# The gate/up loop of the last feed-forward: Silu and the up product one group apart, the up scale folded into the row maximum

## The reference, cut to what matters

```python
def _act_quant(x):
    scale = 127.0 / jnp.clip(jnp.max(jnp.abs(x), axis=-1, keepdims=True), 1e-05)
    xq = jnp.clip(jnp.round(x * scale), -128.0, 127.0) / scale
    return xq
...
gate = jax.nn.silu(_bitlinear(x, w_gate))     # x: 2048 x 1024, w: 4096 x 1024
up = _bitlinear(x, w_up)
g = _silu(_bitlinear(gate * up, w_down))      # w_down: 1024 x 4096
x = x + s * g
```

## Time and profile before

| | us |
|---|---|
| median of two runs | 6970.99 |
| the two runs | 6939.39, 7002.58 |
| profiled execution | 6944.18 |
| its span on the slowest core (core 0) | 6942.6 |
| spans of the eight cores | 6880.7 to 6942.6 |
| stage P9 in it, from 4256 to the end | 2687 |

### The profile page before, as it was taken

The page is one execution under the profiler, slowest core; times in us unless marked ns, Lnnn a source line. Parts: engine busy times, 40 slices in busy tenths (PEclk is TensorE's granted clock), DMA queues, the critical chain, the costliest instruction groups (busy, mean ns, idle before and its releaser), DMA issues.

```text
span 6942.6 us, 51492 instructions; the slowest of 8 cores (6880.7 to 6942.6 us)
## 1 busy us (share of the span) xinstructions
PE 2878.7 (41%) x14444; PEld 1414.7 (20%) x14539; DVE 3893.9 (56%) x5192; ACT 944.2 (14%) x1715; POOL 101.6 (1%) x140
## 2 busy tenths in 40 slices
PE   1455553777710000566666765150505050413221
PEld 0122221333300000132111113140404040313121
DVE  5444435111146567125766664867685959585866
ACT  0000000111101110005555550000000000000000
POOL 0000000000000000000000000000000000000000
PEclk6777766888855555787777778685857585857665
DMA  3200001876667651110000004231313140504131
GB/s 97 43 7 7 13 6 26 124 117 120 125 185 233 210 181 49 27 22 5 19 7 19 19 7 125 70 110 51 116 45 120 41 136 25 161 20 141 49 100 40
DMA packets 360992, 523.49 MB, mean 75 GB/s; under 512 B 21744, under 2 KB 257296, under 8 KB 352528
## 3 DMA queue, kind: packets, MB, share of 16 engines
q1 hardware_dynamic: 268496, 417.43, 19.0%
q0 software_dynamic: 92224, 102.77, 9.6%
HBM read 566.26 MB, written 50.33 MB: 89 GB/s over the span
## 4 chain that ended last, share of the span: by engine, by line
DVE 44%; PE 28%; DMA 16%; issue 6%; ACT 3%; DVEq 1%; SPq 1%; POOL 0%; ACTq 0%; POOLq 0%
DVE sb_BF L1797 7%; DVE sb_BF L1802 7%; PE ps L1392 5%; PE ps L1590 3%; DVE sb_STAT L1433 3%; DMA sb_BF<-s_sp 3%; PE ps L1407 2%; PE ps L1237 2%; DMA sb_BF<-wu0T 2%; PE ps L548 2%; PE ps L1438 2%; DMA sb_FW<-wd1T 2%; PE ps L924 2%; PE ps L916 2%; DMA sb_FW<-wg1T 2%
## 5 line engine op out<-in xcount | busy, mean ns | idle before, releaser
L1684 PE MATMUL ps<-sb_BF 128*128 128x256 bf16 x2048 | 500.1, 287 | 1639.1 <-DVE sb_SCR L1709 1267.5
L1684 PEld LDWEIGHTS ps<-sb_BF 128*128 128x128 bf16 x2048 | 210.1, 103 | 1722.7 <-issue 1689.6
L1419 ACT ACTIVATE sb_BF<-ps 128x512 bf16<-128x512 f32 x1024 | 525.7, 596 | 249.6 <-PE ps L1407 249.3
L1797 DVE SCALAR_TENSOR_TENSOR sb_BF<-sb_BF,sb_FW 128x2048 bf16<-128x2048 bf16 x224 | 513.4, 2292 | 23.6 <-DVE sb_BF L1802 0.5
L1802 DVE SCALAR_TENSOR_TENSOR sb_BF<-sb_BF 128x2048 bf16<-128x2048 bf16 x224 | 513.4, 2292 | 23.3
L1692 PE MATMUL ps<-sb_BF 128*128 128x256 bf16 x2048 | 499.2, 287 | 0.0
L1392 PE MATMUL ps<-sb_BF 128*65 128x512 bf16 x1024 | 411.5, 433 | 22.5 <-ACT sb_BF L1419 13.9
L1706 ACT ACTIVATE sb_SCR<-sb_SCR 128x256 f32<-128x256 f32 x256 | 106.6, 416 | 1957.5 <-DVE sb_SCR L1701 1957.5
L548 PE MATMUL ps<-sb_BF 128*128 128x512 bf16 x1002 | 242.5, 394 | 313.7 <-DMA sb_BF<-wkT 118.8
L916 PE MATMUL ps<-sb_BF 128*128 128x512 bf16 x736 | 298.3, 405 | 146.1 <-DMA sb_BF<-wu0T 54.3
L1590 PE MATMUL ps<-sb_BF 128*128 128x256 bf16 x2048 | 232.5, 275 | 209.3 <-DVE sb_BF L1806 207.2
(11 more groups left out here) (172 smaller groups left out, 4420.3 us busy)
## 6 DMA issues: line engine op xcount, KB each, us to landing
sb_BF<-wgq_sc SPq DMA_DIRECT2D x64, 1024.0 KB, 5.8
sb_BF<-wuq_sc SPq DMA_DIRECT2D x64, 1024.0 KB, 8.7
sb_BF<-wdq_sc SPq DMA_DIRECT2D x32, 2048.0 KB, 14.2
sb_FW<-wg1T SPq DMA_DIRECT2D x32, 1024.0 KB, 6.4
sb_FW<-wu1T SPq DMA_DIRECT2D x32, 1024.0 KB, 6.6
sb_FW<-wd1T SPq DMA_DIRECT2D x64, 512.0 KB, 3.7
sb_FW<-x SPq DMA_DIRECT2D x96, 256.0 KB, 6.1
sb_BF<-wg0T POOLq DMA_DIRECT2D x24, 1024.0 KB, 10.6
```

The source lines that it names most:

```text
L1419: e.activation(ring[rsl], self.bank(bsl, TT), AF.Exp, scale=0.125),
L1684: par=par, c0=c0, last=last: e.matmul(self.bank(bg, TQ), g_s[par][:, k * 512 + mh * 128: k * 512 + (mh + 1) * 128], xq[k][:, c0:c0 + TQ], ...
L1797: e.scalar_tensor_tensor(gbuf, rbuf, sbit, u, ALU.add, ALU.is_le),
```

## The change

Four things change in the loop and its tail.

- Silu of a group and the rest of its VectorE work are one group apart. After the matmuls of group `hh`, VectorE scales its gate half (now line 1729), ScalarE starts Silu, and VectorE turns to group `hh - 1`: it multiplies the up half straight from PSUM by the Silu result (L1676), takes the absolute value (L1682) and folds it into the maximum (L1686). `flush_h` holds these three. Scratch tiles are doubled, in free columns of `MU`.
- The up scale `cu` is no longer multiplied in per group. It is the same for all hidden features of a token, so it is applied once to the row of maxima (L1776), and to the reciprocal (L1785). Only one partition of it is computed.
- The reciprocal is taken on one partition of 256 columns (L1782) in place of 128, and is broadcast together with the maxima by a matmul of 512 columns (L1790). `rec_h` becomes a copy (L1800).
- The weight loads wait for TensorE's last matmul on the buffer, no longer for VectorE's maximum.

```diff
+        self._p9_vp = [0, 0]
...
+            pend = {}
+
+            def flush_h(hh):
+                bu, s_tt = pend.pop(hh)
+                self.drain("vector")
+                self.wait("vector", "se", s_tt)
+                vp = self.emit("vector", lambda e, hh=hh, bu=bu:
+                               e.tensor_tensor(
+                                   hpt[hh], self.bank(bu, TQ),
+                                   sl_s[hh % 2], ALU.mult), inc="ve")
+                self.release_bank(bu, "ve", vp)
+                self._p9_vp[hh % 2] = vp
+                self.drain("vector")
+                self.emit("vector", lambda e, hh=hh: e.scalar_tensor_tensor(
+                    vab, hpt[hh], -1.0, hpt[hh], ALU.mult, ALU.max),
+                    inc="ve")
+                self.drain("vector")
+                self.emit("vector", lambda e: e.tensor_tensor(
+                    mxh, mxh, vab, ALU.max), inc="ve")
+                self.drain("vector")
...
-                    self.wait("sync", "ve", g_cons[par])
+                    self.wait("sync", "te", g_cons[par])
...
-                    self.emit("vector", lambda e, bg=bg: e.tensor_tensor(
-                        scrq, self.bank(bg, TQ), cg, ALU.mult), inc="ve")
-                    v_t = self.milestone("vector", "ve")
-                    self.release_bank(bg, "ve", v_t)
-                    self.wait("scalar", "ve", v_t)
-                    s_tt = self.emit("scalar", lambda e: e.activation(
-                        scr2, scrq, AF.Silu), inc="se")
-                    self.wait("vector", "se", s_tt)
-                    self.emit("vector", lambda e, bu=bu: e.tensor_tensor(
-                        scrq, self.bank(bu, TQ), cu, ALU.mult), inc="ve")
-                    v_t = self.milestone("vector", "ve")
-                    self.release_bank(bu, "ve", v_t)
...
+                    vg = self.emit("vector", lambda e, bg=bg, hh=hh:
+                                   e.tensor_tensor(
+                                       sl_g[hh % 2], self.bank(bg, TQ),
+                                       cg, ALU.mult), inc="ve")
+                    self.release_bank(bg, "ve", vg)
+                    self.wait("scalar", "ve", vg)
+                    if self._p9_vp[hh % 2] > 0:
+                        self.wait("scalar", "ve", self._p9_vp[hh % 2])
+                    s_tt = self.emit("scalar", lambda e, hh=hh: e.activation(
+                        sl_s[hh % 2], sl_g[hh % 2], AF.Silu), inc="se")
+                    pend[hh] = (bu, s_tt)
+                    if (hh - 1) in pend:
+                        flush_h(hh - 1)
+                g_cons[par] = self.cnt["te"]
                 if tq > 0 and hs % 2 == 1:
                     emit_down_strip(tq - 1, hs // 2)
+            for hh in sorted(pend):
+                flush_h(hh)
...
+            self.emit("vector", lambda e: e.tensor_tensor(
+                mrow2, mrow, cu0, ALU.mult), inc="ve")
+            self.drain("vector")
             self.emit("vector", lambda e: e.tensor_single_scalar(
-                mrow, mrow, 1e-5, ALU.max), inc="ve")
+                mrow2, mrow2, 1e-5, ALU.max), inc="ve")
+            self.drain("vector")
+            self.emit("vector", lambda e: e.reciprocal(rfrow, mrow2),
+                      inc="ve")
+            self.drain("vector")
+            self.emit("vector", lambda e: e.tensor_tensor(
+                rfrow, rfrow, cu0, ALU.mult), inc="ve")
...
-                self.bank(0, TQ), self.ONEC[0:1, :], mrow,
+                self.bank(0, 2 * TQ), self.ONEC[0:1, :],
+                self.MU[0:1, 1024:1024 + 2 * TQ],
...
-            v_t = self.emit("vector", lambda e: e.reciprocal(
-                rec_h, self.bank(0, TQ)), inc="ve")
+            v_t = self.emit("vector", lambda e: e.tensor_copy(
+                rec_h, self.bank(0, TQ, off=TQ)), inc="ve")
```

More of the change, by code:

```diff
@@ L191, in build @@
         self.FW = sb("FW", [P, 8192], F32)
-        self.MU = sb("MU", [P, T], F32)
+        self.MU = sb("MU", [P, max(T, 1792)], F32)
         self.RS = sb("RS", [P, T], F32)
@@ L1554, in P9_l1_ffn @@
         mrow = self.MU[0:1, 0:TQ]
+        mrow2 = self.MU[0:1, 1024:1024 + TQ]
+        rfrow = self.MU[0:1, 1280:1280 + TQ]
         scrq = self.SCR[:, 0:TQ]
         scr2 = self.SCR[:, 256:512]
+        sl_g = [self.SCR[:, 0:TQ], self.MU[:, 512:768]]
+        sl_s = [self.SCR[:, 256:512], self.MU[:, 768:1024]]
+        vab = self.MU[:, 1536:1536 + TQ]
+        cu0 = self.STAT[0:1, 256:256 + TQ]
         NS = L1_HID // 512
@@ L1656, in P9_l1_ffn @@
             self.emit("vector", lambda e, c0=c0: e.tensor_scalar(
-                cu, self.SXR[:, c0:c0 + TQ], self.mclip[:, 1:2], 1.0 / 127.0,
-                ALU.mult, ALU.mult), inc="ve")
+                cu0, self.SXR[0:1, c0:c0 + TQ], self.mclip[0:1, 1:2],
+                1.0 / 127.0, ALU.mult, ALU.mult), inc="ve")
             self.drain("vector")
```

## The result

| | before | changed |
|---|---|---|
| median, us | 6944.55 (10 runs) | 7026.14 (11 runs) |
| lowest to highest, us | 6935.67 to 7021.08 | 7014.96 to 7046.57 |
| profiled execution, us | 6944.18 | 7018.84 |

The ratio is 1.0104, with a 95% interval of 1.0077 to 1.013: slower by 1%, within the 2% that count as no change. The forecast was 7020 us, a ratio of 1.011 on the profiled base. Some executions of a kernel take longer, with a lower granted clock on the four cores of one die; where that made over 1% (one execution each of experiments 1, 2 and 4), the execution is left out of the medians.

What follows compares the result with a forecast made beforehand. It took VectorE's chain to set the last stage's loop step, with TensorE having slack. Loop 69, first block -3, weights -6 and tail 16 sum to +76 us on 6944: 7020 us, 8 in 10 within 6960 to 7100.

Steps and rivals of the forecast that it cites:

- (a): Loop, VectorE: one multiplication less and Silu hidden; if VectorE set the step, it would fall from 3.23 to 2.26 us.
- (b): Loop, bank release: the late product stops TensorE from running ahead, so the step is 3.18 us against 3.23.
- overlap rival: Loop: TensorE still overlaps because the bank release is not where it was read; about 6720 us, chance 0.06.
- (c): Loop, down strips of 64 matmuls: no longer hidden by TensorE's lead, a step across one takes 8.73 us against 5.91.
- (d): Block start, clock: groups 2 and 3 run slow at 3.6 and 2.8 us, giving steps of 4.89 and 4.08.
- (e): Block loop in total: 9.8 us longer with strips, 69 us in seven blocks; the first block 3 us shorter.
- signs named for being right: Trace signs expected if the forecast held; the one judged is loop windows of about 123 us with strips.
- (f): Loop, weight loads: issued earlier against their use, giving back 6 us (0 to 8).
- (g): Tail once per block: new reciprocal, multiplications and wider broadcast add 2.0 us, eight times 16 us.
- clock rival: Loop: TensorE, waiting between groups, falls to 1.2 GHz, 3.6 us a group instead of 1.90; about 7130 us, chance 0.11.
- no-change rival: Loop: strips stay as hidden as before, with steps of 3.18 and 5.9 us; 6962 us, chance 0.08.

Runs made afterwards that it cites:

- experiment 1: Changed kernel with each group's product right behind its own gate scaling, ahead of VectorE's next wait for TensorE; 6830.8 us, 0.982 of the kernel before.
- experiment 2: Changed kernel with a group's gate and up halves sharing one bank, so four groups are in flight instead of two; 6765.7 us, 0.974 of the kernel before.
- experiment 4: Changed kernel with eight of a down strip's 64 matmuls behind each group, not all in one piece; 6905.1 us, 0.994 of the kernel before.
- experiment 6: Changed kernel with the weight loads waiting for VectorE's maximum again; 7037.9 us, 1.011 of the kernel before.
- experiment 8: Changed kernel with four groups in flight and the down strips spread over the groups; 6785.2 us, 0.975 of the kernel before.
- third experiment: Changed kernel without the one-group lag, each group finished before the next and Silu in the open; 6909.8 us, 0.992 of the kernel before.

## Why the prediction was right

- *(a), (b), the step.* Forecast 3.18, measured 3.18 to 3.19 in nearly every step. Each link is there: 0.60 from gate scaling to product, 0.42 for the product, 1.90 for the group, and 0.26 for the two handovers. Experiments 1 and 2 take away the late release, or what it costs, in two ways and give back 195 and 260 us on the medians. The overlap rival is refuted in the changed kernel and is what the experiments build; with the changed kernel's two buffers it comes to 6831 us (experiment 1) and not to its 6720, since the strip step stays 8.73.
- *(c), the strips.* Forecast 8.73, measured 8.73 in all 21 such steps; experiment 4 confirms it by removing them.
- *(d), the start of a block.* Partly wrong. Group 2 took 3.4 to 3.6 us, as forecast, but group 3 ran at full clock in six of seven blocks, though I had taken 2.8. The first step was 0.34, not 0.60: between two gate scalings stands only a wait for TensorE, already met.
- *(e), the loop.* From a block's first gate scaling to group 31's first matmul: 112.1 to 112.7 us in six blocks and 114.3 in one (group 3 slow), mean 112.6, against 104.1 before. Times seven, 60 us; the forecast had 69 - 6 = 63. One of the signs named for being right does not fit: from first gate scaling to last maximum a loop takes 118.6 us in the mean against 112.0, and not about 123. The 9.8 us counted to group 31's first matmul, and VectorE follows that by 2.0 us now and by 4.9 before.
- *(f), the loads.* Close in its sum. The loop before does have late weights, in one block above all (the fourth): TensorE idles 3.84 us ahead of group 12 and 4.47 ahead of group 20, and both groups then take 3.6 us.

```profile
5265.90 0.37 PE L1684 MATMUL ps<-sb_BF 128*128 128x256 bf16 x1 [3.84 <-DVE sb_SCR L1701]
```

The view names VectorE, but the banks had been free since 5263.24 (the end of group 10's L1709), and the up weights, issued at 5252.95, landed 12.4 us later, 0.5 us ahead of this matmul. That block's loop is 3.0 us longer than the 103.5 of the block from which I worked, and the mean of the seven is 104.1, so 4 of the 6 us were there to be given back. The changed kernel's loop has no such waits; by experiment 6 it would have none with the later loads either, so the longer step did away with them and not the earlier issue.
- *(g), the tail.* Forecast 2.0 us a block, measured 2.5 in the mean. The rows against the earlier trace rows:

```profile
6045.17 0.41 DVE L1776 TENSOR_TENSOR sb_MU<-sb_MU,sb_STAT 1x256 f32<-1x256 f32 x1 [1.72 <-DMA sb_MU<-sb_SCR]
6045.69 0.28 DVE L1779 TENSOR_SCALAR sb_MU<-sb_MU 1x256 f32<-1x256 f32 x1
6046.07 1.74 DVE L1782 RECIPROCAL sb_MU<-sb_MU 1x256 f32<-1x256 f32 x1
6047.91 0.41 DVE L1785 TENSOR_TENSOR sb_MU<-sb_MU,sb_STAT 1x256 f32<-1x256 f32 x1
6050.73 0.48 DVE L1796 TENSOR_SCALAR sb_MU<-ps,sb_SMALL 128x256 f32<-128x256 f32 x1 [2.40 <-PE ps L1790]
6051.32 0.42 DVE L1800 COPY sb_STAT<-ps 128x256 f32<-128x256 f32 x1
```

The reciprocal of one partition takes 1.74 us (1.76 taken): 128 partitions or one, the columns count. The two multiplications take 0.41 each, not 0.28, which is 0.26 us more together. The other miss is the broadcast, for which VectorE waits 2.40 us. TensorE's timeline has the pair, of the changed kernel and then of the kernel before in two blocks:

```profile
6048.58 2.04 PE L1790 MATMUL ps<-sb_MU,sb_ONEC 1*128 1x512 f32 x2 [5.51 <-DVE sb_MU L1785]
```

```profile
5012.69 1.19 PE L1761 MATMUL ps<-sb_MU,sb_ONEC 1*128 1x256 f32 x2 [2.67 <-DVE sb_MU L1756]
...
6004.47 0.70 PE L1761 MATMUL ps<-sb_MU,sb_ONEC 1*128 1x256 f32 x2 [2.67 <-DVE sb_MU L1756]
```

The changed kernel's pair takes 2.04 in every block, at a granted clock of 0.50. That is near the 1.93 that I had taken. The pair before takes 1.05 to 1.19 us in six blocks (clock 0.50 at 5012.69) and 0.67 and 0.70 in two (1.00 and 0.86), mean 1.04: so +1.00 in the mean, not +0.74. The two misses, 0.26 each, are the 0.5 by which the tail was mis-sized.

- *The clock rival.* The loop's granted clock was 0.98. With idle gaps of 1.28 us, TensorE stayed at 2.4 GHz, as it had at 1.32. The Trainium skill's warning of groups that cycle through banks and make the clock swing (TensorE: Matmul & The Clock Gate, A second HAM failure mode; seen there in another kernel, with 512 columns) is not borne out here: past a block's start, all groups take 1.9 us.
- *The no-change rival* fell with the strips. Its own sum, 6962, left out the 0.05 us by which each of its steps would be shorter, some 9 us.

Sum of the measured parts: 60 + 7 x 2.5 and -1 for the first block, 77 us; the profiled executions differ by 75 and the medians by 82. The mechanism and its size are shown; that the number came within 6 us is in part luck. The forecast stands on the profiled execution, 6944; on the median of the two runs, 6971, it would have been 7047. And the 75 us of the profiles, which are of different cores, hold two differences that nearly cancel and are not the change's: the first gate scaling comes 11.5 us earlier (4271.12 against 4282.63), and an evacuation takes 1.1 us longer in each block (cores of one kernel differ by up to 4 there).

## What to carry to other kernels

When a result's processing is moved one iteration later to hide a latency, ask which buffer is released later by it, and whether a wait for the next iteration now stands ahead of the release. With two buffers, a release one group late makes producer and consumer take turns, and the step becomes the sum of both (1.90 + 1.28) in place of the larger. Keep the release ahead of the next wait, or add a buffer; and put bursts of other work into the idle gaps, not between groups whose consumer has no stock. Where the producer has no gaps left, as with four buffers, spreading the bursts gained nothing (experiment 8).

## What the runs showed of the hardware that was not expected

In the profiles of experiments 1 and 3, the granted clock of some cores lay between the two levels (1.2 and 2.4 GHz) in the mean of whole loops. Windows of the first experiment, core 7, two blocks:

```profile
6103.00:6192.00 89.00, 79.48 (x674) 65.73 (x674) 50.36 (x123) 12.93 (x31) 0.00 (x0) 0.96 0.67 214
6419.00:6516.00 97.00, 91.49 (x672) 71.77 (x673) 51.06 (x123) 12.92 (x31) 0.00 (x0) 0.80 0.60 196
```

In the second of the two, past the start, every group took 2.3 us in place of 1.9 and a strip step 10.2 to 10.5 us; the loop was 8 us longer. Core 6, of the same die, had the like in its last block (a loop of 94.8 us against 87 to 89), but cores 4 and 5, also of that die, did not (87.6 and 87.3 us). In the window of the same times core 0 had 0.97. Cores 4, 6 and 7 of the third experiment show the like (0.82 in one block's loop on core 6). The Trainium skill (TensorE: Matmul & The Clock Gate, Seeing it yourself) tells of a peak-current limit that takes a whole die to 13/16 of its clock, 0.81, when three of its cores run dense matmuls. The size agrees with 0.80 and 0.82, the whole die is not borne out by cores 4 and 5, and no run here shows what caused it. Such a stretch has to be looked for before a difference of some us is put down to an edit.
